# Messages gathered by edge tile instead of by pair tile in a relational graph layer, with every fourth tile's rows kept by the score pass

## What is computed

```python
xl_e = xl[src, edge_type]                       # one row of 4 x 128 floats per edge
xr_e = xr[dst, edge_type]
x = leaky_relu(xl_e + xr_e + e_feat, 0.2)
score = einsum('ehc,ehc->eh', x, att[edge_type])
alpha = softmax of score over the edges with the same dst and edge_type
msg = xl_e.reshape(E, H, C) * alpha[..., None]
agg = segment_sum(msg, dst * R + edge_type)     # then mean over heads, gated sum over r
```

## Time and profile before

| | us |
|---|---|
| median of 3 runs | 9514.06 (9514.05 to 9531.79) |
| the profiled execution | 9592.08, its span 9590.1 |
| busy over the span: PE, VectorE, ScalarE, GpSimd | 5091.3 (53%), 5127.5 (53%), 1979.0 (21%), 5732.0 (60%) |
| transferred | 1155.57 MB, mean 120 GB/s |

### The profile page before, as it was taken

The page is one execution under the profiler, slowest core; times in us unless marked ns, Lnnn a source line. Parts: engine busy times, 40 slices in busy tenths (PEclk is TensorE's granted clock), DMA queues, the critical chain, the costliest instruction groups (busy, mean ns, idle before and its releaser), DMA issues. The chain is left out here.

```text
span 9590.1 us, 93453 instructions
## 1 busy us (share of the span) xinstructions
PE 5091.3 (53%) x23452; PEld 3483.5 (36%) x23571; DVE 5127.5 (53%) x19615; ACT 1979.0 (21%) x5001; POOL 5732.0 (60%) x5738
## 2 busy tenths in 40 slices
PE   2232333444414444497777777777767777623223
PEld 2222322333313333343333333333356766513222
DVE  3333443444424444676777777777766666723235
ACT  0000022222212222310222222222234444500001
POOL 6666526666446666212666666666566666466675
PEclk7555665555555555698999998898979899855556
DMA  2111122222122222187676776676666666221111
GB/s 67 46 46 47 36 46 61 72 68 68 49 60 70 68 69 68 48 328 268 208 210 210 209 214 207 202 209 204 176 168 176 176 176 176 73 54 46 46 46 47
DMA packets 434195, 1155.57 MB, mean 120 GB/s; under 512 B 106036, under 2 KB 147476, under 8 KB 420744
## 3 DMA queue, kind: packets, MB, share of 16 engines
q0 software_dynamic: 295984, 849.83, 32.3%
q1 hardware_dynamic: 122892, 275.01, 8.5%
q10 hardware_dynamic: 14796, 24.75, 0.8%
HBM read 1016.65 MB, written 132.52 MB: 120 GB/s over the span
## 5 line engine op out<-in xcount | busy, mean ns | idle before, releaser
L953 POOL DMA_INDIRECT gat_ring<-gat_table,psrc_idx x1664 | 1641.9, 987 | 1133.2 <-issue 473.1
L589 DVE TENSOR_TENSOR acc<-acc,bank 128x129 f32 (+1 forms) x1664 | 480.2, 289 | 1480.9 <-remote 1333.1
L1939 POOL DMA_INDIRECT pair<-right_table,idx_r_idx x782 | 790.6, 1011 | 636.8 <-PE bank L1978 195.6
L1148 DVE TENSOR_TENSOR acc<-acc,bank 128x130 f32 x1664 | 482.4, 290 | 1209.0 <-remote 869.9
L2099 POOL DMA_INDIRECT msg<-left_table,pidx_idx x832 | 798.3, 960 | 505.4 <-issue 203.0
L1939 POOL DMA_INDIRECT acc<-left_table,idx_l_idx x782 | 812.0, 1038 | 330.4 <-issue 201.1
L521 POOL DMA_INDIRECT gcn_sum_ring<-gcn_table,src_idx x782 | 787.3, 1007 | 371.8 <-issue 227.6
L521 POOL DMA_INDIRECT gin_sum_ring<-in_x,src_idx x782 | 766.2, 980 | 353.2 <-issue 227.0
L1017 PE MATMUL bank<-gat_ring,gat_hot 128*128 128x130 f32 x3328 | 770.7, 410 | 363.8 <-DVE gat_hot L1137 257.1
L2001 ACT ACTIVATE positive<-acc 128x512 f32<-128x512 f32 x782 | 492.3, 630 | 1981.3 <-DVE acc L2029 1354.6
L1978 PE MATMUL bank<-pair,ident 128*128 128x512 f32 x1564 | 860.0, 633 | 1.0 <-issue 0.2
(11 more groups left out here) (554 smaller groups left out, 9362.2 us busy)
## 6 DMA issues: line engine op xcount, KB each, us to landing
gat_place<-local_rows SPq DMA_DIRECT2D x128, 416.0 KB
left_table<-rel_out SPq DMA_DIRECT2D x49, 1032.0 KB, 5.1
right_table<-rel_out SPq DMA_DIRECT2D x49, 1032.0 KB, 3.9
feat<-attr_rows SPq DMA_DIRECT2D x194, 256.0 KB
gat_ring<-gat_table,psrc_idx POOLq DMA_INDIRECT x1664
types<-type_rows SPq DMA_DIRECT2D x98, 256.0 KB
msg<-left_table,pidx_idx POOLq DMA_INDIRECT x832
gin_sum_ring<-in_x,src_idx POOLq DMA_INDIRECT x782
```

The source lines that it names most:

```text
L953: e.indirect_dma_start(ring[:, at:at + TROW], None, table[:, :], bass.IndirectOffsetOnAxis(ap=ed["psrc"][:, i:i + 1], axis=0)).then_inc(*g ...
L1939: e.indirect_dma_start(to[j % NG][:, n * LROW:(n + 1) * LROW], None, tab[:, :], bass.IndirectOffsetOnAxis(ap=idx[:, i:i + 1], axis=0)).the ...
```

## The change

- The score pass: every fourth tile (i % 4 == 1, 196 of 782) has its left rows stored from the left buffer to the table `kept` (`keep`, on SyncE, two batches behind the loads). VectorE's sum goes to `positive` instead of over the left rows, and ScalarE works in place there; so the left buffer is free at `summed`. GpSimd waits for the store before it gathers into such a buffer again. SyncE stores `x_rows` to `x_kept` in front of batch 1.
- The message pass: it gathers by edge tile, and the kept tiles are loaded by SyncE. The rows lie in the space of `x_rows`, 12 tiles (3 lots of 4). ScalarE multiplies two of the four heads by their weights into a ring `weighted` of 64 tiles with two parts of 128 floats for each; VectorE multiplies and adds the other two (`scalar_tensor_tensor`). PE multiplies one unweighted 0/1 matrix per pair by the two parts, which it finds in the ring by `sum_row`. `pair_w`, its stores and its fetches go; the weights are turned straight from `score`. At the end `x_rows` is loaded back.
- The plan: `pidx` and `weight_row` go, with their matrix work, `sum_row` comes (two more small instructions).

```diff
-def rel_scores(k, c, ed, w, tabs, t, acc, soft):
-    left, right, attr_rows, type_rows = tabs[0:4]
+def is_kept(i):
...
                     for tab, idx, to, got, used in ((right, ed["idx_r"], rights, right_in, edge_made),
-                                                    (left, ed["idx_l"], lefts, left_in, relued)):
+                                                    (left, ed["idx_l"], lefts, left_in, summed)):
                         if j >= NG:
                             e.wait_ge(*used.at((j - NG + 1) * PAIR))
                             e.wait_ge(*lin_added.at(j - NG + 1))
+                        if tab is left and j >= NG and j % 2 == 0:
+                            e.wait_ge(*kept_out[j // 2 % 3].at((j - NG) // 2 // 3 + 1, 16))
...
-                for j in range(-(-TILES // BATCH)):
+                def keep(i):
+                    j, n = divmod(i, PAIR)
+                    e.wait_ge(*left_in[j % NG].at(PAIR * (j // NG + 1), 16))
+                    e.dma_start(kept[i // KEEP * P:(i // KEEP + 1) * P, :], side(lefts, i)
+                                ).then_inc(*kept_out[j // 2 % 3].up(16))
+
+                for j in range(-(-TILES // BATCH) + 2):
+                    for i in range((j - 2) * BATCH, min(TILES, (j - 1) * BATCH)):
+                        if i >= 0 and is_kept(i):
+                            keep(i)
+                    if j >= -(-TILES // BATCH):
+                        continue
                     if j == 1:
                         soft.sync_keys(e, 0, w["keys"], w["types"])
                         soft.sync_lasts(e, w["last_keys"])
+                        e.dma_start(x_kept[:, :], x_rows[:, :]).then_inc(*x_out.up(16))
...
+                e.wait_ge(*x_out.at(1, 16))
+                for n in range(3):
+                    e.wait_ge(*kept_out[n].now())
...
-                    if i >= NA:
-                        e.wait_ge(*scored.at(i - NA + 1))
-                    e.activation(positive[i % NA][:, :], side(lefts, i), ACT.Relu, scale=0.8).then_inc(*relued.up())
+                    pos = positive[i % NA][:, :]
+                    e.activation(pos, pos, ACT.Relu, scale=0.8).then_inc(*relued.up())
...
+                        if i >= NA:
+                            e.wait_ge(*scored.at(i - NA + 1))
                         if i % PAIR == 0:
                             e.wait_ge(*left_in[j % NG].at(PAIR * (j // NG + 1), 16))
                             e.wait_ge(*right_in[j % NG].at(PAIR * (j // NG + 1), 16))
                             e.tensor_tensor(soft.straight_of(cn, n), tail(lefts, j), tail(rights, j), ALU.add
                                             ).then_inc(*lin_added.up())
                         e.wait_ge(*edge_made.at(i + 1))
-                        e.tensor_tensor(xs, xs, k.psum[bank_x[i % NX]][:, 0:HC], ALU.add).then_inc(*summed.up())
+                        e.tensor_tensor(positive[i % NA][:, :], xs, k.psum[bank_x[i % NX]][:, 0:HC], ALU.add
+                                        ).then_inc(*summed.up())
...
-def rel_sum(k, c, ed, left, pair_w, soft, t, acc):
+def rel_sum(k, c, ed, tabs, soft, t, acc, x_rows):
+    left, kept, x_kept = tabs[0], tabs[4], tabs[5]
     with ExitStack() as late:
-        NG, NS, NBANK, FIX, FETCH, TURN = 15, 3, 5, 24, 72, 100
-        rows = [k.sb(f"msg{j}", PAIR * LROW, ctx=late) for j in range(NG)]
-        hot = [k.sb(f"rhot{j}", PAIR * P, ctx=late) for j in range(NS)]
-
...
-        weights_in, stored = k.slots("pool_dma_w", 2), k.slots("w_stored", 2)
...
+        Q, NR, NH, NBANK, FIX, TURN = HQ, 3, 3, 5, 24, 100
+        LOTS, FULL = PAIRS // Q, -(-TILES // Q)
+        weighted = k.sb("weighted", RT * 2 * F, ctx=late)
+        rows = [x_rows[:, j * LROW:(j + 1) * LROW] for j in range(NR * Q)]
+        hot = [soft.val, soft.ex, soft.step]
+        weight = [soft.near01, soft.tot]
+        got, kept_in = k.slots("pool_dma", NR), k.slots("kept_in", NR)
...
+        size = lambda b: min(Q, TILES - b * Q)
+        group_of = lambda i: divmod(i + FRONT, P)
+        row_of = lambda i: rows[i % (NR * Q)]
+        part_of = lambda i, j: weighted[:, (i % RT * 2 + j) * F:(i % RT * 2 + j + 1) * F]
+
+        def weight_of(i, h):
+            g, m = group_of(i)
+            n, m = divmod(m, SPAN)
+            u, j = divmod(m, RUN)
+            col = j * P + n * 32 + h * NRUN + u
+            return weight[g % 2][:, col:col + 1]
...
-                for i in range(PAIRS):
-                    j, n = divmod(i, PAIR)
-                    if i == NG * PAIR:
-                        fetch(0)
-                    g, where = part_of(i)
-                    if where == FETCH and g + 1 < G:
-                        fetch(g + 1)
-                    if n == 0 and j >= NG:
-                        e.wait_ge(*product.at(j - NG + 1))
-                    e.indirect_dma_start(
-                        rows[j % NG][:, n * LROW:(n + 1) * LROW], None, left[:, :],
-                        bass.IndirectOffsetOnAxis(ap=ed["pidx"][:, i:i + 1], axis=0)).then_inc(*got[j % NG].up(16))
+                for i in range(TILES):
+                    b = i // Q
+                    if i % Q == 0 and b >= NR:
+                        e.wait_ge(*mixed.at(b - NR + 1))
+                    if not is_kept(i):
+                        e.indirect_dma_start(
+                            row_of(i), None, left[:, :],
+                            bass.IndirectOffsetOnAxis(ap=ed["idx_l"][:, i:i + 1], axis=0)).then_inc(*got[b % NR].up(16))
...
-                for g in range(SGROUPS):
-                    if g >= 2:
-                        e.wait_ge(*stored[g % 2].at(16 * (g // 2), 16))
-                    e.wait_ge(*fixed.at(g + 1))
-
-                    for n in range(4 if g else 2):
-                        store(e, g, n)
-                for j in range(2):
-                    e.wait_ge(*stored[j].at(16 * len(range(j, SGROUPS, 2)), 16))
+                for i in range(TILES):
+                    b = i // Q
+                    if is_kept(i):
+                        if b >= NR:
+                            e.wait_ge(*mixed.at(b - NR + 1))
+                        e.dma_start(row_of(i)[:, 0:HC], kept[i // KEEP * P:(i // KEEP + 1) * P, :]
+                                    ).then_inc(*kept_in[b % NR].up(16))
+                e.wait_ge(*mixed.at(FULL))
+                e.dma_start(x_rows[:, :], x_kept[:, :]).then_inc(*x_back.up(16))
+                e.wait_ge(*x_back.at(1, 16))
...
-                e.wait_ge(*fixed.at(1))
-                for n in (2, 3):
-                    store(e, 0, n)
                 put(0)
-                for j in range(NBATCH):
-                    g, where = part_of(j * PAIR)
-                    if where == 0 or j == 0:
+                for b in range(FULL):
+                    g, where = group_of(b * Q)
+                    if where == 0 or b == 0:
                         e.wait_ge(*placed.at(g + 1))
-                    if where == TURN + 2 and g + 1 < G:
+                    if where == TURN + Q and g + 1 < SGROUPS:
+                        if g:
+                            e.wait_ge(*mixed.at(b - TURN // Q))
                         put(g + 1)
-                    e.wait_ge(*hot_made.at(j + 1))
-                    if j >= NS:
-                        e.wait_ge(*product.at(j - NS + 1))
-                    for n in range(PAIR):
-                        for h in (2, 3):
-                            m = e.mul(hotw[j % NS][n][:, h * P:(h + 1) * P], hot[j % NS][:, n * P:(n + 1) * P],
-                                      weight_of(j * PAIR + n, h))
-                    m.then_inc(*scaled_s.up())
+                    e.wait_ge(*got[b % NR].at(b // NR * (Q - 1) + size(b) - 1, 16))
+                    e.wait_ge(*kept_in[b % NR].at(b // NR + 1, 16))
+                    free = b * Q + size(b) - 1 - RT + NB
+                    if free > 0:
+                        e.wait_ge(*product.at(-(-free // Q)))
+                    for i in range(b * Q, b * Q + size(b)):
+                        for j in range(2):
+                            h = 2 * j + 1
+                            m = e.mul(part_of(i, j), row_of(i)[:, h * F:(h + 1) * F], weight_of(i, h))
+                    m.then_inc(*scaled.up())
 
             @block.tensor
             def _(e):
                 def turn(g):
-                    e.wait_ge(*weights_in[g % 2].at(g // 2 + 1, 16))
+                    e.wait_ge(*fixed.at(g + 1))
                     if g:
                         e.wait_ge(*placed.at(g))
-                    for h in range(H):
-                        m = e.transpose(k.psum[BANK_T][:, h * P:(h + 1) * P], by_pair[g % 2][:, h * P:(h + 1) * P],
-                                        c["ident"][:, :])
...
-                for j in range(NBATCH):
-                    g, where = part_of(j * PAIR)
-                    if where == TURN and g + 1 < G:
+                for b in range(LOTS):
+                    g, where = group_of(b * Q)
```

(69 more changed lines are left out.)

79 lines of the change are left out of this document (30 added, 49 removed).

## The result

| | us |
|---|---|
| before, median of 4 runs | 9519.36 (9514.05 to 9531.79) |
| after, median of 4 runs | 9280.72 (9267.28 to 9292.2) |
| ratio | 0.9747, 95% interval 0.9727 to 0.9767 |
| the profiled execution after | 9271.48, its span 9269.7 |

The change gains 2.5%, 239 us on the medians; 152 was predicted.

What follows compares the result with a forecast made beforehand. The prediction took a full transfer queue of gathered rows, not an engine, to bound both passes. Message pass -221, stores +58 and x_rows store +11 gave -152 us, from 9514 to 9362 us; range 9250 to 9510.

Steps and rivals of the forecast that it cites:

- Message pass, -221: Message pass: gathering by edge tile, with 196 tiles by plain load, ends it at 8045 instead of 8266, 221 us gained.
- The lot: Message pass, four tiles: gathers 4.50 us, plain load 0.30, hiccups of the shallower ring 0.3, together 5.1 us.
- The tail: End of message pass: 12 lots remain because pairs run up to 49 behind the tiles; at 3 us each, 36 us.
- A full transfer queue with a fixed rate: Score and message passes: gathered rows set the time, not an engine; 1.50 us per 264 KB gather, 176 GB/s.
- Coupling of 0.2 bytes lost per byte, +58 us for the stores: Score pass: each byte stored takes 0.2 bytes from the gathers, so 51.4 MB of stores cost 58 us.
- Store of x_rows, +11: Score pass start: 3.2 MB stored on SP in front of batch 1 lengthens VectorE's wait before its first sum, 11 us.
- Plan, 0: Plan: taking out the third index table and weight rows is hidden by the first pass's first gathers, gaining nothing.
- Rival A: Both passes: a packet on SP's queue costs the gathers its full time; result +36, about 9550 us; chance 0.1.
- Rival B: Message pass: three-lot ring too shallow or its chain serial, 5.7 us per lot, 117 us lost, about 9480; chance 0.22.
- Rival C: Message pass falls to VectorE's own pace, 4.4 us per lot, stores at 0.1; -318, about 9200 us; chance 0.08.
- Rival D: Score pass: late feat loads and store waits do show, some 150 us, about 9510, no change; chance 0.12.
- The cover that the prediction named: Score pass: 24 queued gathers (36 us) hide late feat loads and store waits; without it, 3 us per batch, 290 us.

Runs made afterwards that it cites:

- combo: Kernel after with four lots of rows, release tile by tile, and the x_rows store behind the third batch's loads; slow gathers: 9411.2 us, 0.9808 of kernel before.
- before_again: Kernel before, unchanged, run and profiled again in a session with slow gathers: 9607.89 us, ratio 1.0009.
- ring2: Kernel after with the message pass's ring of rows holding two lots instead of three; slow gathers: 9536.54 us, 0.9928 of kernel before.
- quad: Kernel after with each kept tile stored four times, three into tables nobody reads; slow gathers: 9402.53 us, 0.9791 of kernel before.
- nostore: Kernel after without the stores of kept tiles, loading 196 tiles of the left table instead; fast gathers: 8171.6 us, 0.9817 of kernel before.
- control: Kernel after, unchanged, run again in a session with fast gathers: 8169.77 us, 0.9807 of kernel before.
- twice: Kernel after with each kept tile stored twice, the second time where nobody reads; fast gathers: 8168.16 us, 0.9808 of kernel before.
- half: Kernel after with every other tile kept instead of every fourth, 391 stores and kept loads; fast gathers: 8146.83 us, 0.9784 of kernel before.
- gatherall: Kernel after with all 782 tiles of the message pass gathered, none stored or loaded; fast gathers: 8329.31 us, 0.9999 of kernel before.
- after_again: Kernel after, unchanged, run again with fast gathers, the same run as the control: 8169.77 us, 0.9807 of kernel before.

## Why the prediction came near, and which steps were wrong

- **Message pass, -221: measured -261.** The head is right: 46 us from the first gather to the end of the first lot, as worked out. The lot was put at 5.1 us and 0.08 for mending; from 6931.7 to 7910.3 us it took 5.02. The tail was put at 36 and took 31. These are 31 and 5 of the 40 us. But the 5.1 was right by luck. It was made of 3 x 1.50 + 0.30 us of transfer and 0.3 for hiccups, with 4.1 for VectorE hidden behind it. What the lot consisted of is VectorE's own 4.28 us and 0.74 of its waits, most of it for PE's banks (82.1 of the 95.9 us in the window).
- **"A full transfer queue with a fixed rate": wrong, shown.** The pace of about 1.50 us per gather is real, its reason isn't bytes. In the gathers of the first layer, 66 KB each, the same session gives (1146.0 - 18.6) / 781 = 1.44 us per gather at 46 GB/s. Over the whole message pass the gather queue moved 67120 packets for 832 gathers and 7 fetches of weights, 80 each. At 7505 us of the earlier trace rows it had moved 28410: without the four fetches up to there, 351 gathers of the 352 issued. So of the 30 that VectorE had not used, the rows of at least 29 were there; PE, which uses them first, had worked through 326 pairs (2611 matmul records, 8 per pair). The share of 0.64 of the transfer engines pointed the same way, and I read over it.
- **Coupling of 0.2 bytes lost per byte, +58 us for the stores: nothing measurable.** This follows from the wrong step: what doesn't wait for bytes loses nothing to bytes. 51.4 MB went with 2 us (combo against before_again, both with slow gathers) to 12 (ring2), and four times as much with 29. This is the mis-sized term. The score pass 40 to 90 us longer, which the prediction named as a sign of being right, did not come.
- **Store of x_rows, +11: 10.25 us**, by which the wait in front of the first sum grew; of that wait, the later store in combo took away 6. **Plan, 0:** nothing of it is seen.
- With the stages' own numbers, -261 + 0 + 10 = -251, against 239 in the medians, whose interval is 19 us either way.
- **Rival A**, packets that take their full time, is refuted: quad's 154 MB would have cost over 400 us and went with 27. The rule on which it stood (the Trainium skill, "DMA: Bandwidth & Descriptors", Queues, rings and completion order: an engine drains one packet of one queue before it turns to the next) is not refuted by that. By it a packet is delayed only where others are queued in front of it, and no backlog of gathers was found where packets were counted (the message pass above, the first layer below); in the score pass they weren't counted, its share of 0.70 to 0.87 leaves room.
- **Rival B**, the ring too shallow: not with three lots, but near. GpSimd's waits are B's sign (134.6 us for VectorE), but VectorE isn't short of rows, and the lot isn't B's 5.7. Two lots give 5.91. With fast gathers three lots cost 0.15 us per lot against four.
- **Rival C**, VectorE's own pace: with fast gathers it is what happens, at 4.26 to 4.41 us per lot (4.4 was its number). In the first comparison it is most of the lot, with the waits for PE's banks on top. I had put it at 0.08.
- **Rival D**, late loads of feat: with fast gathers VectorE's waits for them grow from 34.3 us in 2 waits (nostore) to 75.1 in 10 (control), 88.6 in 19 (twice) and 116.1 in 20 (half), and the time doesn't, since the gathers in front cover them. The cover that the prediction named was there.

In sum: the sign held in both kinds of session, but that the size of the main term came near is luck. 1.50 us per gather was the pace of a pass in which VectorE waited for PE's banks, read as the pace of the transfers; multiplied by three gathers it came near a lot that is made of something else. The same reading gave the 58 us, and there it had nothing to cancel it.

What isn't shown: which part of the change brings the 261 us with slow gathers. gatherall, which leaves the kept rows out, ran with fast gathers only, and with fast gathers they are the whole gain. With slow gathers it could be as well that PE hands over 208 banks instead of 416, for which VectorE had waited 204.7 us between 7150 and 7800 us of the kernel before; no run separates the two.

## What to carry to other kernels

Count gathers before bytes: with fast gathers, where GpSimd's issue was the bound, what helped is 196 gathers fewer, fetched as plain loads of rows that an earlier pass had in its buffers anyway; at a share of the transfer engines of 0.75 to 0.86 with the stores, the traffic for it cost nothing that could be measured. Before a wait is put down to a full queue, compare the packets moved with the gathers issued, look for the same pace at another row size, and count which engine has really gone how far. When a gather bound is lifted, work out the next engine's floor at once: VectorE stood at 4.3 us per lot, below GpSimd's 5.16, so a deeper ring or twice as many kept rows were worth only 25 us more. The version with four lots, or that with the release by tile (0.978 each), beats both kernels with fast gathers, the kernel after by 0.3%; with slow gathers no gain of the two together was seen.

## What was not expected of the hardware

The same program on the same chip took 8330 us in one session and 9604 us in another. Every gather pass is slower in the slow kind, whatever its row size; single instructions are not (a multiply-add of 128x128 takes 0.34 us in both). The first layer shows it best. VectorE there, slow gathers (after, first comparison) and below it fast gathers (after_again):
```profile
591.21 1.26 DVE L579 TENSOR_TENSOR acc<-acc,bank 128x129 f32 x4 [13.52 <-remote]
592.38 0.68 DVE L558 TENSOR_TENSOR gin_sum_hot<-node_iota,e_local 128x512 f32<-128x512 f32 x1
...
605.91 1.26 DVE L579 TENSOR_TENSOR acc<-acc,bank 128x129 f32 x4 [12.84 <-remote]
```
```profile
597.36 1.26 DVE L579 TENSOR_TENSOR acc<-acc,bank 128x129 f32 x4 [3.42 <-PE bank L542]
598.54 0.69 DVE L558 TENSOR_TENSOR gin_sum_hot<-node_iota,e_local 128x512 f32<-128x512 f32 x1
601.59 1.27 DVE L579 TENSOR_TENSOR acc<-acc,bank 128x129 f32 x4 [2.37 <-PE bank L542]
```
And the transfers in the slow case, 1 us each (last two columns: share of the transfer engines, GB/s):
```profile
602.00:603.00 1.00, 0.00 (x0) 0.00 (x0) 0.00 (x0) 0.00 (x0) 0.00 (x0) 0.50 0.28 66
603.00:604.00 1.00, 0.00 (x0) 0.00 (x0) 0.00 (x0) 0.00 (x0) 0.00 (x0) 0.50 0.00 0
604.00:605.00 1.00, 0.00 (x0) 0.00 (x0) 0.00 (x0) 0.00 (x0) 0.00 (x0) 0.50 0.00 0
605.00:606.00 1.00, 0.00 (x0) 0.00 (x0) 0.09 (x1) 0.00 (x0) 0.00 (x0) 0.50 0.00 0
```
At 605 us 400 gathers were issued there and 320 tiles added; 13248 packets had been moved, which is 400 gathers of 32 and the 448 of other small transfers. (The whole pass, 782 gathers, ends at 25472, the same 448 more.) So nothing was left to transfer. With fast gathers 446 were issued by then and 440 added.

Nor does PE, which uses the rows first, wait for them. PE of the same stretch, its matmuls up to 592 us, and GpSimd's next gather:
```profile
577.82 2.08 PE L542 MATMUL bank<-gin_sum_ring,gin_sum_hot 128*128 x8 [6.30 <-issue]
593.26 2.08 PE L542 MATMUL bank<-gin_sum_ring,gin_sum_hot 128*128 x8 [13.36 <-issue]
L542 PE MATMUL bank<-gin_sum_ring,gin_sum_hot x648: 272/422/579, 150.1 to 579.5; 128*128 x162
606.05 0.95 POOL L511 DMA_INDIRECT gin_sum_ring<-in_x,src_idx  x1 [4.66 <-remote]
```
A lot of four tiles is 8 of these matmul records (1664 for the 208 lots of the pass). 648 are 81 lots, the 81st from 577.82 to 579.90 us, at once behind its 0/1 matrix of 577.00. The 320 tiles added are 80 lots, so the additions from 605.91 us are those of the 81st: VectorE, idle since 593.06, takes up 26 us later what PE's records show as done. GpSimd goes on at 606.05; by the program its next gather needs the same mark of PE, that 81 lots are multiplied. The same with fast gathers:
```profile
595.14 2.08 PE L542 MATMUL bank<-gin_sum_ring,gin_sum_hot 128*128 x8 [3.20 <-DMA gin_sum_ring<-in_x,src_idx]
```
It ends at 597.22 and VectorE adds from 597.36. Over all 208 lots, from the end of a lot's last matmul record to its first addition, it is 0.13 us in the median and 1.5 at most with fast gathers, 1.9 in the median and 36 at most with slow ones. There PE waits for rows ("DMA"); with slow gathers it has them and its successors wait. In the profiles of fast sessions no wait is "remote".

So the name "slow gathers" is wrong as an explanation. What comes late is neither the data nor PE's start on it, but the moment at which VectorE and GpSimd learn that PE is done with a lot. That fits the message pass, where the lot is VectorE's pace and its waits for PE's banks. Whether PE's work itself ends late (the ends of its records are modelled) or only the news of it, and what makes a session one or the other, no run here shows.
